# Six-deep rings and paired landing waits in the two network passes of a graph-network kernel

## The reference

```
def _propagate(h, edge_attr, edge_index, We, be, Wl):
    x_i = h[edge_index[0]]
    x_j = h[edge_index[1]]
    x_edge = jnp.concatenate([x_i, x_j, edge_attr], axis=-1)
    x_edge = _mlp1(x_edge, We, be)          # silu(x @ W + b)
    x_edge = edge_attr @ Wl * x_edge
    x_p = _seg_mean(x_edge, edge_index[0], h.shape[0])
    return x_p + h
```

## Time and profile before

| | before |
|---|---|
| median of 3 runs | 16309.38 us (16301.63 to 16316.3) |
| the profiled execution, its own time | 16222.93 us |
| its span in the trace | 16221.2 us |
| first and last gather of pass 0 | 7210.7 and about 10016 us |
| first and last gather of pass 1 | about 10228 and 13034.2 us |
| POOL busy over the span | 9525.9 us (59%) |
| PE, DVE, ACT busy over the span | 9592.5, 7215.4, 3844.3 us |

### The profile page before, as it was taken

How to read it: one execution, slowest core, us unless ns; L and a number is a source line. 1 busy time by engine, 2 the same in 40 slices (tenths; PEclk the granted TensorE clock), 3 DMA queues, 4 the chain that set the end, 5 groups by cost and what they waited for, 6 DMA issues and landing times.

```text
span 16221.2 us, 180153 instructions
## 1 busy us (share of the span) xinstructions
PE 9592.5 (59%) x40895; PEld 6450.1 (40%) x40896; DVE 7215.4 (44%) x18628; ACT 3844.3 (24%) x8556; POOL 9525.9 (59%) x8465
## 2 busy tenths in 40 slices
PE   0466657766478878845555556655555545555555
PEld 0111122221133333335555554555555545555554
DVE  8876657777000000013333332333333357777776
ACT  0344444442011111112222222222222212222221
POOL 0378878888645434426666664566666645555553
PEclk9999999999688778865555555555555555555555
DMA  9922222222599989992222223222222344444444
GB/s 385 358 15 19 19 15 20 20 20 18 168 342 370 343 306 357 359 113 86 84 86 84 85 84 50 75 84 86 84 86 85 80 95 139 141 141 140 140 139 96
DMA packets 1483063, 2197.01 MB, mean 135 GB/s; under 512 B 882955, under 2 KB 926027, under 8 KB 1454669
## 3 DMA queue, kind: packets, MB, share of 16 engines
q1 hardware_dynamic: 907628, 1490.52, 28.2%
q0 software_dynamic: 453120, 343.50, 12.7%
q10 hardware_dynamic: 121698, 356.43, 6.0%
HBM read 1771.19 MB, written 419.98 MB: 135 GB/s over the span
## 4 chain that ended last, share of the span: by engine, by line
POOL 40%; DMA 22%; issue 21%; PE 8%; DVE 4%; another core or an unknown queue 3%; ACT 1%; POOLq 0%; SPq 0%; DVEq 0%; ACTq 0%
POOL gat L645 18%; POOL adj L613 12%; POOL arena L645 8%; DMA arena<-adj 8%; DMA gat<-q_table,ring_i 6%; DMA arena<-h_table,ring_i 5%; PE bank L1029 5%; DMA adj<-put_n,put_at 2%; POOL rec_src L599 1%; DVE arena L1356 1%; PE same L1161 1%; PE same L1000 1%; DVE arena L1358 1%; PE same L980 0%
## 5 line engine op out<-in xcount | busy, mean ns | idle before, releaser
L645 POOL DMA_INDIRECT gat<-q_table,ring_i x3456 | 3626.6, 1049 | 2405.7 <-DMA gat<-q_table,ring_i 1025.0
L613 POOL DMA_INDIRECT adj<-put_n,put_at x1632 | 2559.9, 1569 | 1265.3 <-DVE put_at L1440 638.1
L1183 PE MATMUL bank<-onehot_t,onehot 128*128 128x64 f32 x6912 | 1585.5, 424 | 2574.9 <-DVE acc L1578 1880.5
L1183 PEld LDWEIGHTS bank<-onehot_t,onehot 128*128 128x128 f32 x6912 | 1506.7, 330 | 2653.8 <-DVE acc L1578 1938.5
L599 POOL DMA_INDIRECT rec_src<-pay,ring_i x1632 | 1606.4, 984 | 1566.9 <-ACTq L743 1093.2
L645 POOL DMA_INDIRECT arena<-h_table,ring_i x1728 | 1729.4, 1001 | 1346.2 <-DMA arena<-h_table,ring_i 760.8
L1088 PE MATMUL same<-onehot 32*128 32x512 f16 x3264 | 1678.6, 615 | 620.0 <-DVE onehot L1411 389.3
L1029 PE MATMUL bank<-arena,hs 128*64 128x512 f32 x5880 | 1596.0, 707 | 508.2 <-DMA arena<-adj 506.9
L1419 DVE TENSOR_SCALAR_CACHE_REDUCE onehot<-same 128x128 bf16<-128x128 f32 (+3 forms) x1632 | 1233.0, 756 | 843.2 <-PE same L1090 675.9
L1173 PE MATMUL bank<-hs,arena 128*128 x6912 | 1564.0, 421 | 29.3 <-ACT arena L867 29.3
L1173 PEld LDWEIGHTS bank<-hs,arena 128*128 128x128 f32 x6912 | 1525.9, 333 | 29.8 <-issue 29.8
(11 more groups left out here) (277 smaller groups left out, 13003.2 us busy)
## 6 DMA issues: line engine op xcount, KB each, us to landing
arena<-adj SPq DMA_DIRECT2D x300, 2560.0 KB
arena<-rec_src SPq DMA_DIRECT2D x432, 552.0 KB
adj<-hs ACTq DMA_DIRECT2D x25, 6656.0 KB, 46.3
rec_src<-pay ACTq DMA_DIRECT2D x1, 119232.0 KB, 332.0
arena<-lo_row SPq DMA_DIRECT2D x432, 256.0 KB
hs<-b_row SPq DMA_DIRECT2D x108, 1024.0 KB
acc<-b_row SPq DMA_DIRECT2D x108, 1024.0 KB
gat<-q_table,ring_i POOLq DMA_INDIRECT x3456
```

The source lines that it names most:

```text
L613: nc.gpsimd.indirect_dma_start(counts, bass.IndirectOffsetOnAxis(put_at[:, b // 3 % 4, c:c + 1], 0), put_n[:, b // 3 % 4, c:c + 1], None, ...
L645: nc.gpsimd.indirect_dma_start(rows[n][:, u, :], None, table, bass.IndirectOffsetOnAxis(ring_i[:, n, u:u + 1], 0)).then_inc(landed[n], 16)
L1183: last = mm(bank[6 + n % 2][:, u // 2 * D:(u // 2 + 1) * D], onehot[:, n % 2, u, :], msg[n % 2][:, u, :], start=u % 2 == 0, stop=u % 2 == 1)
```

## The change

It makes the rings of the two network passes six groups deep (`R = 6`) instead of four: gathered rows, records, low digits, and their semaphores, with the loops of all five engines running over six groups. Of the gathered rows, slots 4 and 5 lie in `pay`, and the ring of low digits moves from `arena` to `h`. POOL waits for landed gathers only ahead of every second group (`burst=2`), and then issues 16 gathers without such a wait. SP issues the loads of two groups at a time, and it now also waits for the gathers of the group before the two to have landed. The attention network calls `gathers` with the default, and keeps its waits.

```
-                for n in range(4):
+                for n in range(R):
                     load_edges(k, 0, n)
-                with sp.Fori(1, NG // 4) as i:
-                    for n in range(4):
-                        sp.wait_ge(l_msg, i * 4 + (k * NG + n - 3 + OFF))
-                        sp.wait_ge(l_oht, i * 4 + (k * NG + n - 3 + OFF))
+                with sp.Fori(1, NG // R) as i:
+                    for n in range(0, R, 2):
+                        hold(sp, l_gat[(n - 1) % R], i * (16 * U) + (k * (NG // R) + (n > 0)) * 16 * U)
+                        hold(sp, l_msg, i * R + (k * NG + n + 2 - R + OFF))
+                        hold(sp, l_oht, i * R + (k * NG + n + 2 - R + OFF))
                         load_edges(k, i, n)
+                        load_edges(k, i, n + 1)
...
-            def gathers(table, rows, landed, i, n, before, first):
-
-                if not first:
+            def gathers(table, rows, landed, i, n, before, first, burst=1):
+
+                if not first and n % burst == 0:
                     hold(pool, landed[(n - 1) % len(landed)], i * (16 * U) + before)
...
             def node_rows(k, i, n, first=False):
-                hold(pool, l_idx, i * 4 + (k * NG + n + 1))
-                gathers(q_table[k], gat4, l_gat, i, n, (k * (NG // 4) + (n > 0)) * 16 * U, first)
+                hold(pool, l_idx, i * R + (k * NG + n + 1))
+                gathers(q_table[k], gat_in, l_gat, i, n, (k * (NG // R) + (n > 0)) * 16 * U, first, burst=2)
...
-        gat4 = [gat_flat[:, n * U * D:(n + 1) * U * D].rearrange("p (u d) -> p u d", u=U) for n in range(4)]
+        pay_flat = pay[:].rearrange("p q u r -> p (q u r)")
+        gat_in = [(gat_flat if n < 4 else pay_flat)[:, n % 4 * U * D:(n % 4 + 1) * U * D].rearrange("p (u d) -> p u d", u=U)
+                  for n in range(R)]
...
+        lo_bc = [h_flat[:, n * U * P // 2:(n + 1) * U * P // 2].bitcast(BF16) for n in range(R)]
```

More of the change, by code:

```diff
@@ L38 @@
 OFF = 4
+R = 6
 LAG = 8
@@ L364, in build @@
         l_idx = sem("l_idx")
-        l_gat = [sem(f"l_gat{n}") for n in range(4)]
-        l_pay = [sem(f"l_pay{n}") for n in range(4)]
-        l_lo = [sem(f"l_lo{n}") for n in range(4)]
+        l_gat = [sem(f"l_gat{n}") for n in range(R)]
+        l_pay = [sem(f"l_pay{n}") for n in range(R)]
+        l_lo = [sem(f"l_lo{n}") for n in range(R)]
         l_abs = sem("l_abs")
@@ L883, in propagate_act @@
                 onehot_rows(0, 0)
-                with act.Fori(0, NG // 4 - 1) as i:
-                    for n in range(4):
+                with act.Fori(0, NG // R - 1) as i:
+                    for n in range(R):
                         group(i, n)
-                for n in range(4):
-                    group(NG // 4 - 1, n, 4 - n)
+                for n in range(R):
+                    group(NG // R - 1, n, R - n)
             layer_act(0, "h", FT[1])
@@ L1187, in propagate @@
                 look_up(0, 0)
-                with pe.Fori(0, NG // 4 - 1) as i:
-                    for n in range(4):
-                        look_up(i + (n + 1) // 4, (n + 1) % 4)
+                with pe.Fori(0, NG // R - 1) as i:
+                    for n in range(R):
+                        look_up(i + (n + 1) // R, (n + 1) % R)
                         sums(i, n)
-                for n in range(4):
-                    if n < 3:
-                        look_up(NG // 4 - 1, n + 1)
-                    sums(NG // 4 - 1, n)
+                for n in range(R):
+                    if n < R - 1:
+                        look_up(NG // R - 1, n + 1)
+                    sums(NG // R - 1, n)
             def ft(c, j):
@@ L1588, in group @@
                     if not first:
-                        gather_sums(i - 1 if n == 0 else i, (n - 1) % 4)
-                for n in range(4):
+                        gather_sums(i - 1 if n == 0 else i, (n - 1) % R)
+                for n in range(R):
                     index(0, n)
@@ L1594, in propagate @@
                 edge_part(0, 0)
-                for n in range(4):
+                for n in range(R):
                     group(0, n, first=n == 0)
-                with dve.Fori(1, NG // 4 - 1) as i:
-                    for n in range(4):
+                with dve.Fori(1, NG // R - 1) as i:
+                    for n in range(R):
                         group(i, n)
-                for n in range(4):
-                    group(NG // 4 - 1, n, more=False, last=n == 3)
-                gather_sums(NG // 4 - 1, 3)
+                for n in range(R):
+                    group(NG // R - 1, n, more=False, last=n == R - 1)
+                gather_sums(NG // R - 1, R - 1)
             def residual(j, n, other):
```

79 lines of the change are left out of this document (39 added, 40 removed).

## The result

The changed kernel takes 15661.42 us (median of 3 runs, 15658.15 to 15672.9) against 16309.38 us: a ratio of 0.9605, with a 95% interval from 0.9583 to 0.9626.

A forecast was written before the change was run, and what follows sets the result against it. The prediction took POOL's gathers and their landing waits to bound the network passes. Savings of 379 + 18 + 108 = 505 us from 16309.4 gave 15804 us, with a range of 15690 to 15960 us.

The forecast's parts named there:

- the third term of the sum: Network passes: POOL's gathers held up less by DVE's two-input instructions, 108 us saved, 40 to 170 allowed.
- The moved loads: SP's later loads, two groups at a time behind a landing: cost nothing, give or take 5 us.
- Landing waits: POOL in the network passes: 206 waits dropped, each becoming a 0.40 us gap, 379 us saved (307 to 400).
- Padding groups: Last 8 groups of each pass: the fixed 2.24 us of a wait goes once per pair, 18 us (0 to 48).
- The layout by hand: Hand-timed pair of groups in the new kernel: DVE holds up gathers about 1.1 us a pair, against 1.64 before.
- The port: Rival: DVE's two-input instructions hit POOL's gathers in full, 4.2 us a pair, giving 16462 us; 3%.
- The network's chain: Rival: late low digits make the pair's work overrun its free 8 us and set the pace, near 16020 us; 4%.
- Landings did not pile up: Answers the rival that 16 gathers in a row need twice the end wait, 4.5 us, giving 16180 to 16300 us; 4%.
- Waits halved to 214: Sign: POOL's waits for landed gathers halve to about 216, the regular ones still near 2.2 us.
- The gap of 0.3 to 0.75: Sign: POOL's gap between the two groups of a pair is 0.3 to 0.75 us.
- Mean gather between 0.99 and 1.03: Sign: POOL's mean gather time in the network passes is between 0.99 and 1.03 us.
- The first gather behind a landing near 0.95: Sign: POOL's first gather after a landing wait takes near 0.95 us and not 1.36.

The follow-up runs named there:

- the repeats: The kernel before and the changed kernel, each run once more unchanged; ratios 1.0001 and 0.9602 to the kernel before.
- pool_pairs: The changed kernel, but SP loads one group at a time without waiting for landed gathers; ratio 0.9704 to the kernel before.
- pairs_no_hold: The changed kernel without SP's wait for landed gathers, loads still going out for two groups at a time; ratio 0.9721 to the kernel before.
- loads_pairs: The changed kernel with POOL waiting for landings ahead of every group (`burst=1`), SP's loads as in the change; ratio 0.9853 to the kernel before.
- burst3: The changed kernel with POOL's landing wait ahead of every third group in the network passes; ratio 0.948 to the kernel before.
- attention_pairs: The changed kernel with the landing wait ahead of every second group in the attention stage too; ratio 0.9357 to the kernel before.

## Why the prediction was wrong

The direction and the mechanism were right; the third term of the sum, gathers held up by DVE, was mis-sized, 108 us for a measured 247 to 260. The moved loads, a step that I had cost at nothing, carry most of it.

- *Landing waits: right.* 379 us were forecast. Measured are 485 us of waits less 67 of new gaps, 418, for this term and the padding together, against 379 + 18. Of the 418 the padding groups have 29 (next point) and the regular ones 389. A new gap is 67 / 215 = 0.31, near the lower bound, and not the 0.40 that I took, which gives 206 x 0.09 = 19 us more. The waits that are left are a little longer, 2.27 in the mean against 2.23, which takes 8 of them back. So sixteen gathers in a row lengthen the wait at their end by no more than 0.04 us.
- *Padding groups: right within their bounds, the size low.* Their landing waits are 102.3 us before, over both passes, and 71.1 in the change; less 8 gaps of 0.3 that is 29 us against 18. With the gathers that are no longer held up, both stretches (from the start of the first padding gather to that of the last) are 35 us shorter.
- *Gathers held up by DVE: the term that failed.* 108 us were forecast, 40 to 170 allowed; measured are 260 in the first profiles, 247 in the repeats (3621.7 to 3374.7). Of the 247, 71 come with POOL's pairs alone (3621.7 to 3550.3, pool_pairs) and 176 with SP's wait (3550.3 to 3374.7). The layout by hand gave 1.1 us of hits in a pair; the profile has (3366.6 - 3456 x 0.944) / 216 = 0.48. Two of its lines were too dear. "It hits one gather by up to 0.5", of the message: it came when the layout had it, but mostly between two starts, and holds up the seventh gather in 30 pairs of 108, 0.09 us a pair. "Two hits of 0.3 in the mean", for the train of L1550, edge_part and message: in the pair shown it hits once (1.26 at 8523.54), and the next gather starts at the seam between two instructions (8525.11, 0.94); over the pass it is 71 hits in 108 pairs, 0.2 us a pair. One line was too cheap: the following one-hot columns, or the edge_part behind them, don't always fall within the landing wait. In 49 pairs of 108 they reach into the next pair's first gather (1.45 at 8530.78), 0.2 us a pair. The cheap line takes back part of the dear ones: that the term came out no further off is luck.
- *A reading that was wrong without harm.* "So a gather that starts under such an instruction does nothing until about 0.1 us behind its end." The gather of 8534.91 ends at 8536.27, 0.81 behind the end of L1568 (8535.46), and a whole one takes 0.947: it is 0.13 us further than that, not 0.1 behind. The price of a hit, at most 0.53, was read from the durations and doesn't change.
- *Moved loads, "I cost this at nothing".* For the network's own chain that was right: the longer waits of ACT, PE and DVE did not reach POOL. But SP's wait for the landing is what sends the message away from POOL's first gathers, and pool_pairs and pairs_no_hold price it at 1.0 to 1.2% of the time, 160 to 195 us, loads_pairs at 1.5%. I had put part of this into the layout and didn't see that it was a term of its own, which could have been bounded on its own.
- *The range.* I had both ends of the third term, 352 gained and 550 lost, and cut them to 40 to 170 because "phases that are fixed by the landing make neither end likely". Fixed phases speak for an end as much as against it. With the 352 that I had worked out, 400 + 48 + 352 = 800, the range would have reached 15509 and held the result. With what was measured, 389 + 29 + 260 = 678, the sum gives 15631; the 30 us from there to 15661 are about what the attention stage gained.
- *The rivals.* The port did not take the gain; the gathers were held up less than before, not more. The network's chain did not become the bound (POOL waits for no indices within a pass, and burst3 runs faster still). Landings did not pile up.
- *The signs in the profile.* Waits halved to 214, right. The gap of 0.3 to 0.75, right at its end. Mean gather between 0.99 and 1.03: wrong, 0.974. The first gather behind a landing near 0.95: only in about half of the pairs, 1.16 in the mean. Regular groups at 11.7 us: 11.33.

The 648 us of the medians are then 660 to 690 in the passes less some 40 in the attention stage. I had also leaned on one profiled execution in which attention happened to be 165 us shorter than in its repeat; as that stage was left out of the sum, no term suffered from it.

## What to carry to other kernels

When one engine issues many small DMAs and sets the pace, price each wait for a landing as a whole pause of that engine, and ask if it guards anything: here every second one went, then two of three, and in another stage three of four, until another chain, a row of scores on its way through HBM and back, set the pace. To see that a second chain has caught up, read the chain of waits and not only the engine's own waits: in attention_pairs POOL still waited for landings 107 times, and the chain had already left it. Then look at what other engines do at the moment at which that engine starts again: work released by the same landing runs into it, and to delay that work by a few microseconds (here by letting loads wait that did not need to) was worth 1.0 to 1.5%. Where a cost hangs on phases, keep both of its ends in the range.

## What the runs showed of the hardware

- A gather that starts under a DVE instruction with two SBUF inputs ends 0.82 us behind that instruction's end, where a free one takes 0.944. In the kernel before, up to 9700 us, all 386 gathers of 1.05 us or more do so, within 0.81 to 0.85; in the change all 160 of pass 0, within 0.81 to 0.86. None of them stands away from such an instruction, and node_part, which has one input in PSUM, holds up none (L1568 at 8519.74 in the change starts 0.05 us before a gather, which takes 0.94). A gather that is under way when the instruction starts is not held up.
- The reverse is nearly free. None of the 1728 such instructions of the kernel before (L1550, L1558, L1568) takes more than 0.695 us, though 197 of those up to 9700 us start within a gather. Where a gather and L1573 start within 0.01 us of each other (8525.10 in the change), L1573 takes 0.73 and the gather its 0.94. The section "Who interferes with whom" of the Trainium skill's page "SBUF — State Buffer" has the second instruction wait until the first has finished; here DVE lost 0.04 us to a gather of 0.94.
- The same program on the same data takes 2969.5 or 3134.1 us in two executions for a stage bound by landing waits (760.8 against 962.8 us of them). One profile is not enough to price a stage to 5%.
- Rings of six rather than four in the network passes go with 37 to 46 us more in an attention stage that does not use them. It was seen on both chips that had kernels of either depth, with one four-deep profile on each, and is not explained.
